# Two found tiles per group in both layers, the first search ahead of the projection, its mask ahead of the addition

## The reference

```python
h = jnp.maximum(_layernorm(x, axis=-1), 0.0)
x = x + _L0_gnn_ref(h, edge_index, edge_weight1, edge_attr_3, edge_attr_5, L0_gnn_W)
h = jnp.maximum(_layernorm(x, axis=-1), 0.0)
x = x + _L1_gnn_ref(h, L1_gnn_weight, L1_gnn_w_comp, L1_gnn_self_loop_weight, ..., src, dst, edge_type_86)
```

## Time and profile before

| | us |
|---|---|
| median of 3 timed runs | 3520.62 |
| profiled execution | 3504.08 |
| its span, first to last instruction | 3502.3 |
| layer 0: first gather to last gather issued | 26.29 to 1739.95 |
| layer 1: first gather to last gather issued | 1803.56 to 3444.12 |

### The profile page before, as it was taken

One profiled execution on the slowest core, in us unless ns is written; L12 is line 12 of the kernel. 1 busy time (PEld: TensorE's weight loads), 2 busy tenths in 40 slices (PEclk: granted clock), 3 DMA queues, 4 the chain that ended last, 5 costly groups with the idle time before them and its releaser, 6 DMA issues. The chain is left out here.

```text
span 3502.3 us, 110849 instructions
## 1 busy us (share of the span) xinstructions
PE 3104.4 (89%) x42844; PEld 2581.4 (74%) x42844; DVE 2749.0 (78%) x4092; ACT 883.5 (25%) x1910; POOL 2353.0 (67%) x2481
## 2 busy tenths in 40 slices
PE   3999999999999999999978888888888888888887
PEld 2777777777777777777767777777777777777776
DVE  7777777777777777777768888888888888888886
ACT  1001001001001001001034443334444444444443
POOL 5666666666666666666537777777777777777772
PEclk9999999999999999999969999999999999999998
DMA  4111111111111111111123333333333333333331
GB/s 130 26 23 25 25 23 25 25 23 25 25 23 25 25 23 25 25 23 25 23 67 57 54 55 56 56 56 56 55 57 57 57 56 56 57 57 56 56 57 39
DMA packets 218214, 149.97 MB, mean 43 GB/s; under 512 B 121914, under 2 KB 199003, under 8 KB 217821
## 3 DMA queue, kind: packets, MB, share of 16 engines
q0 software_dynamic: 79232, 40.73, 11.8%
q1 hardware_dynamic: 138013, 100.79, 11.7%
q10 hardware_dynamic: 576, 2.40, 0.2%
HBM read 135.47 MB, written 8.22 MB: 41 GB/s over the span
## 5 line engine op out<-in xcount | busy, mean ns | idle before, releaser
L538 POOL DMA_INDIRECT xg<-h_table,idx x2476 | 2342.1, 946 | 1091.5 <-issue 721.3
L606 PE MATMUL ps<-h,blocks 128*128 128x448 f32 x9100 | 1921.0, 369 | 23.1 <-DVE blocks L947 23.1
L606 PEld LDWEIGHTS ps<-h,blocks 128*128 128x128 f32 x9100 | 1692.7, 188 | 229.4 <-issue 78.4
L947 DVE TENSOR_TENSOR blocks<-scratch,ps 128x896 fp32r<-128x896 int16 x650 | 703.0, 1082 | 117.1 <-PE ps L606 113.1
L1038 DVE TENSOR_TENSOR Z<-coef,ps 128x864 f32<-128x864 f32 (+1 forms) x522 | 734.3, 1448 | 16.6 <-DVE ps L979 0.2
L672 PE MATMUL ps<-Z,xg 128*32 128x32 f32 (+3 forms) x25008 | 505.9, 215 | 4.9 <-DVE Z L1038 4.9
L826 ACT ACTIVATE p_left<-ps 96x128 f32<-96x128 f32 (+2 forms) x262 | 64.3, 245 | 1734.9 <-PE ps L642 1617.6
L1056 DVE TENSOR_TENSOR aggT<-aggT,ps 64x128 f32 (+1 forms) x262 | 74.1, 283 | 515.0 <-PE ps L654 515.0
L672 PEld LDWEIGHTS ps<-Z,xg 128*32 128x32 f32 x25008 | 403.8, 110 | 88.8 <-issue 67.6
L956 DVE SCALAR_TENSOR_TENSOR scratch<-ramp_sb,scratch,ps 128x448 f32<-128x448 f32 x650 | 438.3, 674 | 0.2
L961 DVE TENSOR_REDUCE xg<-scratch 128x32 f32<-128x448 f32 x650 | 402.7, 620 | 22.3
(11 more groups left out here) (105 smaller groups left out, 1048.7 us busy)
## 6 DMA issues: line engine op xcount, KB each, us to landing
xg<-h_table,idx POOLq DMA_INDIRECT x2476, 2.4
rows_b<-typ_short SPq DMA_DIRECT2D x130, 258.0 KB
scratch<-q_short SPq DMA_DIRECT2D x260, 96.0 KB, 3.3
rows_b<-dst_short SPq DMA_DIRECT2D x130, 126.0 KB
coef<-in_edge_dram SPq DMA_DIRECT2D x130, 54.0 KB, 1.9
att_tab<-p_table SPq DMA_DIRECT2D x393, 8.1 KB
p_table<-Z SPq DMA_DIRECT2D x8, 297.0 KB, 3.8
X<-in_x_dram SPq DMA_DIRECT2D x7, 224.0 KB, 5.0
```

Of the source, the lines that this page charges most:

```text
L538: pool.indirect_dma_start(xg[:, g.q, t - g.s * J, :], None, h_table[n], bass.IndirectOffsetOnAxis(ap=idx[:, t:t + 1], axis=0)).then_inc(L. ...
L606: last = pe.matmul(found_ps[b], blocks[:, b, c, :], h_2[:, a, c], start=(c == 0 and a == 0), stop=(c == NCH - 1 and a == 1))
L947: dve.tensor_tensor(blocks[:, b], q_b[:, g.b, NPM - NP[n] + i, :].unsqueeze(1).broadcast_to([P, NCH, P]), block_ps.unsqueeze(2).broadcast_ ...
```

## The change

`NP` becomes a number for each layer and buffer `q`, all of them 2: layer 0 now gathers ten tiles of a full group and finds two, as layer 1 does. `NPM`, the number of tiles that have an entry in `q_b`, goes from 3 to 2. The counts of the semaphores are computed by a new function, `tiles_before`. On PE the first tile of a group is found ahead of the projection and the second behind it; on DVE the mask of the first tile is built ahead of the addition. The order changes in both layers.

```diff
-NP = [3, 2]
-NPM = max(NP)
+NP = [[2, 2, 2, 2], [2, 2, 2, 2]]
+NPM = max(max(np) for np in NP)
...
+    def tiles_before(self, n, later=0):
+
+        r = self.r + later
+        of_pass = FULL // 4 * sum(NP[n]) + sum(NP[n][0:FULL % 4])
+        return self.k * of_pass + (self.i + r // 4) * sum(NP[n]) + sum(NP[n][0:r % 4])
...
-                    wait(sp, L.block_set, (g.full_order() - 2) * NP[n])
+                    wait(sp, L.block_set, g.tiles_before(n, -1))
...
                 def step(gs):
+                    tiles = gs[0].found_tiles(n) if gs[0] else []
+                    find_rows(tiles[0:1])
                     if gs[2]:
                         project(gs[2])
-                    if gs[0]:
-                        find_rows(gs[0])
+                    find_rows(tiles[1:])
...
-                def found_rows(new, old):
-
-                    old_tiles = old.found_tiles(n) if old else []
+                def found_rows(new, old, back):
+
+                    old_tiles = old.found_tiles(n)[-2:] if old else []
                     new_tiles = new.found_tiles(n) if new else []
-                    for i in range(max(len(old_tiles), len(new_tiles))):
-                        if new_tiles:
+                    for i in range(max(len(old_tiles), len(new_tiles), 1)):
+                        if i < len(new_tiles):
                             block_rows(new, new_tiles[i])
-                        if i < 2 and old_tiles:
-                            pick_rows(old, old_tiles[i - 2 if NP[n] > 1 else 0])
-                        if i >= 2 and new_tiles:
+                        if i == 0 and back:
+                            add(back)
+                        if i < len(old_tiles):
+                            pick_rows(old, old_tiles[i])
+                        if 2 <= i < len(new_tiles):
                             pick_rows(new, new_tiles[i - 2])
...
                 def step(gs):
-                    if gs[3]:
-                        add(gs[3])
-                    found_rows(gs[0], gs[1])
+                    found_rows(gs[0], gs[1], gs[3])
```

More of the change, by code:

```diff
@@ L86 @@
 assert NOWHERE < 1 << 15 and NREL <= 1 << 8
-assert NCH * MC == M and FULL % 2 == 0 and JT <= JH and PS <= P
+assert NCH * MC == M and FULL % 2 == 0 and all(sum(np) % 2 == 0 for np in NP) and JT <= JH and PS <= P
 def gathers_of_pass(n, q):
-    return len(range(q, FULL, 4)) * (J - NP[n]) + (JT if q == FULL % 4 else 0)
+    return len(range(q, FULL, 4)) * (J - NP[n][q]) + (JT if q == FULL % 4 else 0)
 class Group:
@@ L120, in halves @@
         return -(-self.nj // JH), min(self.nj, JH) * WN
-    def full_order(self):
-        return self.k * FULL + self.s + 1
     def full_order2(self):
@@ L133, in gathers @@
             return gathers_of_pass(n, self.q)
-        return (self.i + self.r // 4 + 1) * (J - NP[n])
+        return (self.i + self.r // 4 + 1) * (J - NP[n][self.q])
     def gathered_tiles(self, n):
-        return self.nj if self.tail else J - NP[n]
+        return self.nj if self.tail else J - NP[n][self.q]
+    def tiles_before(self, n, later=0):
+        r = self.r + later
+        of_pass = FULL // 4 * sum(NP[n]) + sum(NP[n][0:FULL % 4])
+        return self.k * of_pass + (self.i + r // 4) * sum(NP[n]) + sum(NP[n][0:r % 4])
     def found_tiles(self, n):
@@ L143, in found_tiles @@
             return []
-        return [(i, J - NP[n] + i, (self.b * NP[n] + i) % 2, (self.full_order() - 1) * NP[n] + i + 1) for i in range(NP[n])]
+        np = NP[n][self.q]
+        return [(NPM - np + i, J - np + i, (sum(NP[n][0:self.q]) + i) % 2, self.tiles_before(n) + i + 1) for i in range(np)]
 def unit(u):
@@ L597, in edge_sums, with find_rows @@
                 weights = w0c if n == 0 else w1_sb
-                def find_rows(g):
-                    for i, j, b, o in g.found_tiles(n):
+                def find_rows(tiles):
+                    for i, j, b, o in tiles:
                         pe.wait_ge(L.block_set, o)
@@ L663, in sum_edges @@
                     if not g.tail:
-                        pe.wait_ge(L.picked, g.full_order() * NP[n])
+                        pe.wait_ge(L.picked, g.tiles_before(n, 1))
                     pe.wait_ge(L.Z_set, g.order() * 2 - 1)
@@ L946, in block_rows @@
                     wait(dve, L.found, o - 2)
-                    dve.tensor_tensor(blocks[:, b], q_b[:, g.b, NPM - NP[n] + i, :].unsqueeze(1).broadcast_to([P, NCH, P]),
+                    dve.tensor_tensor(blocks[:, b], q_b[:, g.b, i, :].unsqueeze(1).broadcast_to([P, NCH, P]),
                                       block_ps.unsqueeze(2).broadcast_to([P, NCH, P]), ALU.is_equal).then_inc(L.block_set, 1)
@@ L952, in pick_rows @@
                     i, j, b, o = tile
-                    u = g.s * NPM + NPM - NP[n] + i
+                    u = g.s * NPM + i
                     dve.wait_ge(L.found, o)
@@ L1003, in scores @@
                     if not g.tail:
-                        dve.wait_ge(L.picked, g.full_order() * NP[n])
+                        dve.wait_ge(L.picked, g.tiles_before(n, 1))
                     dve.wait_ge(L.ex_done, o)
```

## The result

| | before | after |
|---|---|---|
| median of the timed runs, us | 3521.82 | 3353.52 |
| lowest to highest, us | 3517.32 to 3525.52 | 3353.24 to 3354.56 |
| profiled execution, us | 3504.08 | 3353.24 |

The ratio is 0.9523, with a 95% interval of 0.9507 to 0.954: 168 us faster. The forecast was 3371, in a range of 3350 to 3415.

What follows compares the result with a forecast made beforehand. PE bounded layer 0, PE and POOL side by side layer 1; POOL would bound both. Gains of 113.2 and 36.3 us, 149.5 together, off the median 3520.62 (16.5 us above the profiled execution) gave 3371 us, range 3350 to 3415.

Steps and rivals of the forecast that it cites:

- 16.5 us carried over: Whole kernel: the median of runs before lies 16.5 us above the profiled execution, cause unknown, and this was added to the forecast.
- layer 1's gain: End of layer 1: with POOL as the bound, the sums of group 129 come 36.3 us earlier.
- Layer 0 at POOL's floor: Layer 0: ten gathers at 1.248 us make POOL's step 12.48 us; last group's sums start at 1653.8, 113.2 us earlier.
- PE's step of 10.2 in layer 0: Layer 0: sums, wait, two searches and projection take PE 10.2 us, 2.3 under POOL's 12.48.
- The exchange of waits: Both layers: PE's wait for ScalarE (0.91 and 1.46 us) becomes one for DVE's pick, 0.78 and 0.8 us.
- Layer 1's step of 11.9: Layer 1: the shorter wait cuts PE's step by 0.66 us, from 12.55 to 11.9, so POOL bounds this layer too.
- threshold: Layer 1: PE's step must average 12.27 us for PE to catch up with the gain of 36.3 us.
- rival (a): Layer 1 gains nothing, the wait for the pick replacing that for ScalarE, step 12.5 us: 3407 us, chance 0.12.
- POOL's lead: Layer 1: POOL runs some three groups ahead of the sums, a lead that a faster PE eats up.
- POOL's pauses: First half of layer 1: 543 gathers go from 1.271 to 1.248 us each, saving 12 us.
- The address load: Layer 1, DVE: the load now behind the mask costs between 0 and 1.09 us a step; the low bound was taken.
- The clock: Layer 0: gaps of 2.3 us may halve TensorE's clock; POOL stays the bound up to share 0.27; counted as zero.

Runs made afterwards that it cites:

- mixed_b: Changed kernel with layer 0 finding three tiles in every other group, two in the others: 3295.54 us, ratio 0.9379 to the kernel before; as mixed, in the slow condition, 1.0107.
- search_first_b: Changed kernel with DVE's old order, the addition ahead of the first tile's mask: 3527.83 us, ratio 1.0044 to the kernel before.
- nine_b: Changed kernel with nine gathers per full group instead of ten, both layers: 3184.59 us, ratio 0.9063 to the kernel before; as nine, in the slow condition, 0.9616.
- np_only_b: Changed kernel with both old orders, two tiles kept: 3395.73 us, ratio 0.9663 to the kernel before; as np_only, in the slow condition, 1.05.
- warm_b: Changed kernel with eight useless matmuls behind the second search of each layer 0 step: 3357.37 us, ratio 0.9556 to the kernel before.

## Why the prediction was right

The mechanism held: two tiles put layer 0 on POOL's floor, and the order brings layer 1 there for its last third. The sizes of layer 1's step and of the 16.5 us carried over were off, and what makes up layer 1's gain was partly another thing than the forecast took it for.

- **Layer 0 at POOL's floor: right.** The last group's sums start at 1653.66; forecast 1653.8. POOL does not wait for PE. 113.4 us against 113.2.
- **PE's step of 10.2 in layer 0: nearly.** 10.35, by mixed_b. The search is 3.0 to 3.1 us where it stands alone, and not 2.93, a third of a run of 42 matmuls.
- **The exchange of waits: right, within 0.1 us.** 0.67 us in layer 0 and 0.91 in layer 1, forecast 0.78 and 0.8. search_first_b shows on what it hung: with the mask still behind the addition the same wait is 1.72 and 1.86.
- **Layer 1's step of 11.9: wrong by 0.3.** The scores of 88 steps, from 1732.70 to the first that waits for a gather at 2805.89, are 12.20 us apart on average, and nine_b gives 12.18. The forecast read the 12.55 as two bounds side by side. But neither before nor in np_only_b does a score of layer 1 wait for a gather, so POOL didn't hold PE in either. In np_only_b the step is 12.48 (scores from 1732.69 to 3342.34 in 129 steps), as long as POOL's floor; no run with fewer gathers in the old order shows whether that is chance. From there, two terms were mis-sized. The wait fell from 1.37 (177.8/130) to 0.91, so by 0.46 and not by 0.66. And splitting the run of 28 matmuls costs something that the forecast put at nothing: between 1900 and 2500 us the searches keep PE busy for 5.97 us a step in np_only_b (286.8 for 1345 matmuls) and for 6.24 in the changed kernel (308.1 for 1382). Together that would be a saving of 0.2; measured is 12.48 - 12.20 = 0.28. It sufficed, because the threshold was 12.27; the margin was 0.07 and not 0.37, so rival (a) was nearer than its 0.12 says.
- **Layer 1's gain: right in size, in part by luck.** 37.3 us against 36.3. The 24 us of POOL's lead that PE eats up are what the order brings (26.4 by np_only_b). The 12 us of POOL's pauses are not: np_only_b, with the old order, has lost them as well. They belong to the first 52 steps of layer 1 in the profiled execution of before, which were longer; see the 16.5 us below.
- **The address load: right.** The low bound, nothing: the addition still waits 0.86 us for PE.
- **The 16.5 us carried over: wrong.** This is the term that was mis-sized: its true value was nothing. The profiled execution of before plus the sum, 3354.6, is 1.4 us from the profiled execution of after, and the runs of after lie within 1.3 us of each other. In twenty runs of the kernel before, in this condition, the times go from 3490.6 to 3527.3, four from 3490.6 to 3495.0, fifteen from 3517.3 to 3527.3 and one at 3503.1; np_only_b has 3379.7 and 3411.8. All kernels with the new order repeat within 1.0 to 3.2 us, also those in which PE bounds layer 1 throughout (nine_b 2.6, search_first_b 2.3 in eight runs). So the offset doesn't belong to PE as the bound, but to the old order.

  The trace of before shows a place for it. In the first 52 steps of its layer 1 (scores from 1846.19 to 2507.77) a step takes 12.72 us and PE waits 1.61 us in it for ScalarE's copy; in the next 76 (up to 3456.74) it takes 12.49, and PE waits 1.37, as in all of np_only_b's profile, which is the one of 3379.7. Step and wait differ by the same 0.24. An estimate from these figures: with 129 steps of the long kind the profiled execution of before would have taken 3504 + 20 = 3524 us, with none of them 3504 - 10 = 3494, and that is where the two groups of times lie. For np_only_b it gives 129 x 0.24 = 31 us between the two kinds, and its runs are 32 apart. PE's wait for the copy is gone in the new order, and the scatter with it. No run of the long kind was profiled from end to end, so this is not shown; and why the wait has two lengths is open. The granted clock doesn't explain it (0.985 to 0.988 in the sixteen runs beside the experiments).
- **The clock: right.** It fell after some of the gaps of about 2.1 us, as the end of layer 0 had suggested, and came back in the next search. At 0.92 and two levels of 0.5 and 1, half clock took (1 - 0.92)/0.5 = 0.16 of the time, under the 0.27 from which it would have decided. A slow step also cost less than the 18.7 us of the forecast, 12.83 in the step shown above, since the clock came back within its first search (5.12 us and not 5.86). warm_b shows the price: none. The section "Why this matters for your kernels" of the Trainium skill's page "TensorE: Matmul & The Clock Gate", which warns of longer gaps only, did not describe this trace. The measurement decides.

## What to carry to other kernels

Count the instructions of an engine per microsecond, and hold that against its best pace anywhere in the trace: POOL at 74% busy was at its limit, with 1.248 us a gather in layer 0 of four kernels (1122 gathers in 1400 us in the changed one, np_only_b, warm_b and search_first_b). Move work between the two engines until their steps are equal, and no further: two tiles everywhere gave 168 us, and alternating three and two gave 58 more. When a step is moved ahead on one engine, move what it waits for on the other engine too: the search without its mask lost the whole gain. And hold a few microseconds of a profile against a second execution: 12 us of layer 1's gain come from how the profiled execution of the kernel before ran, and not from the change.

## What the runs showed of the hardware

- A fall of TensorE's clock is free where another engine bounds (warm_b, 1.00 against 0.92 at no gain), and goes with longer searches where PE does (search_first_b's layer 1, 0.96: 6.71 us a step against 6.24).
- There is a condition in which the same program takes 4870 to 4945 us instead of 3520. PE stops within runs of small matmuls, for about 1 us on average and up to 2.6 (np_only, L622), ended by nothing recorded. POOL's gathers keep their 0.94 us. With one gather less in each group the step of layer 1 was some 1.5 us shorter there (nine against mixed), though POOL was waiting for PE. The same edit has opposite signs in the two (two tiles in the old order 0.966 and 1.05, the alternating one 0.938 and 1.011), so a comparison holds only beside a run of the kernel before on the same chip in the same job.
